# Moving the stores of the blocks' sums from SyncE to ScalarE in the edge stages of a two-layer graph kernel

## What is computed

```python
h = (x @ W).reshape(n, HEADS, OUT_C)                 # n = 6250, 8 heads of 32
e = leaky_relu(a1[src] + a2[dst], 0.2)               # 206250 edges, sorted by dst
seg_max = segment_max(e, dst, n)
ex = exp(e - seg_max[dst])
denom = segment_sum(ex, dst, n)
out = segment_sum(h[src] * (ex / denom[dst])[:, :, None], dst, n)
```

## Time and profile before

| what | value |
|---|---|
| median of the three runs | 6683.05 us |
| the profiled execution, its span | 7807.0 us |
| first edge stage's steps, by the trace | about 470 to 3178 us |
| second edge stage's steps, by the trace | about 4665 to 7084 us |
| busy over the span | PE 67%, PEld 48%, DVE 42%, POOL 46%, ACT 18% |

### The profile page before, as it was taken

The page is one execution under the profiler, slowest core; times in us unless marked ns, Lnnn a source line. Parts: engine busy times, 40 slices in busy tenths (PEclk is TensorE's granted clock), DMA queues, the critical chain, the costliest instruction groups (busy, mean ns, idle before and its releaser), DMA issues. The chain is left out here.

```text
span 7807.0 us, 99204 instructions
## 1 busy us (share of the span) xinstructions
PE 5257.7 (67%) x19729; PEld 3739.4 (48%) x19729; DVE 3278.9 (42%) x5938; ACT 1371.0 (18%) x2977; POOL 3613.4 (46%) x3708
## 2 busy tenths in 40 slices
PE   2387887788788878228999625556565556663498
PEld 1144444444444444227999514444444444442498
DVE  6255555555555555721111313333333333336244
ACT  2122222222222222002222200000000000000122
POOL 2635555555555554042222056666666666650222
PEclk9689999999999999658999857777777777786699
DMA  6434444444444443515666544444444444434255
GB/s 220 136 101 122 122 119 123 124 124 125 122 123 121 122 124 102 186 60 165 183 183 183 153 102 114 113 115 115 114 112 113 113 114 116 113 102 154 101 198 188
DMA packets 718013, 1022.24 MB, mean 131 GB/s; under 512 B 301733, under 2 KB 531561, under 8 KB 692608
## 3 DMA queue, kind: packets, MB, share of 16 engines
q0 software_dynamic: 183456, 485.95, 23.8%
q1 hardware_dynamic: 527676, 519.31, 21.7%
q10 hardware_dynamic: 6564, 14.14, 0.5%
HBM read 868.26 MB, written 153.27 MB: 131 GB/s over the span
## 5 line engine op out<-in xcount | busy, mean ns | idle before, releaser
L773 POOL DMA_INDIRECT e_rows<-sc_table,e_eidx x3224 | 3115.9, 966 | 2253.8 <-issue 952.6
L880 PE MATMUL e_ps_o<-e_rows,e_oh 128*128 128x264 f32 x6448 | 1918.5, 449 | 856.9 <-ACT e_res L969 700.8
L880 PEld LDWEIGHTS e_ps_o<-e_rows,e_oh 128*128 128x128 f32 x6448 | 1379.2, 222 | 1384.3 <-issue 1147.6
L1064 DVE SCALAR_TENSOR_TENSOR e_u<-e_encr,e_adst,e_ps_hd 128x512 f32<-128x512 f32 x806 | 597.1, 745 | 1160.2 <-remote 366.1
L1132 DVE TENSOR_TENSOR e_rows<-e_rows,e_ps_w 128x1024 f32<-128x1024 f32 x806 | 970.7, 1207 | 106.3 <-issue 83.5
L822 PE MATMUL e_ps_X<-e_u,e_hwide 128*104 128x512 f32 x1612 | 871.1, 635 | 16.8 <-DVE e_u L1064 14.8
L1055 DVE TENSOR_SCALAR e_ohT<-e_at,e_nid 96x512 bf16<-96x512 int16 x806 | 292.5, 363 | 1384.6 <-DMA e_aw<-sc_a2p 553.7
L969 ACT COPY e_res<-e_ps_o 32x264 f32<-32x264 f32 x806 | 296.0, 367 | 3291.4 <-PE e_ps_o L884 1242.4
L810 PE MATMUL e_ps_enc<-e_at,e_w_enc 96*128 96x512 bf16 x806 | 317.9, 394 | 570.6 <-ACT e_encr L942 383.4
L1676 PE MATMUL x_ps_h<-x_xT,x_w 128*128 128x256 f32 x2624 | 648.2, 405 | 15.4 <-DMA x_b<-in_L_ffn_b_dram 15.4
L1676 PEld LDWEIGHTS x_ps_h<-x_xT,x_w 128*128 128x128 f32 x2624 | 638.5, 337 | 20.6 <-issue 16.4
(11 more groups left out here) (290 smaller groups left out, 3538.7 us busy)
## 6 DMA issues: line engine op xcount, KB each, us to landing
x_w<-in_L_ffn_W_dram SPq DMA_DIRECT2D x112, 1024.0 KB
e_at<-sc_grp SPq DMA_DIRECT2D x403, 192.0 KB
x_w<-in_L_ffn_w_dram SPq DMA_DIRECT2D x60, 1024.0 KB
e_rows<-sc_table,e_eidx POOLq DMA_INDIRECT x3224
e_at<-sc_grp SPq DMA_DIRECT2D x403, 96.0 KB
sc_agg<-e_res SPq DMA_DIRECT2D x816, 33.0 KB
sc_xb<-r_zero SPq DMA_DIRECT2D x24, 1032.0 KB
x_xin<-sc_xb SPq DMA_DIRECT2D x86, 258.0 KB
```

Of the source, the lines that this page charges most:

```text
L773: pool.indirect_dma_start(rows[:, k, s, j, :], None, dr["table"][:, :], bass.IndirectOffsetOnAxis(eidx[:, k, s, j:j + 1], 0)).then_inc(s_r ...
L880: nc.tensor.matmul(ps_o[:, 0:ROW], oh[:, k, at_j:at_j + P], rows[:, k, s, j, :], start=(j == 0), stop=False)
L1064: nc.vector.scalar_tensor_tensor(u[:, p, h, :], encr[:, h, :], adst[:, h:h + 1], ps_hd[:, h, :], ALU.add, ALU.mult).then_inc(s_u, 1)
```

## The change

SP loses the store, its two holds, and the third number of each table entry. ACT gets them: after the `evict` of step s it issues the store of step s - 1, whose window start it reads from the table itself. `evict` loses its own hold on `s_out`, since that of the store now covers it. The 31 stores that followed SP's loop become one after ACT's loop.

```diff
@@ SP
             def entry(t):
-                _, vals = nc.values_load_multi_w_load_instructions(tab[0:1, bass.ds(t * 3, 3)], engines=[sp.engine], ...
+                _, vals = nc.values_load_multi_w_load_instructions(tab[0:1, bass.ds(t * 3, 2)], engines=[sp.engine], ...
-            def store(t, s, n):
-                hold(sp, s_out, t * 16 - (32 * SB - OUT0), s_ps)
-                hold(sp, s_ev, t - (BEHIND - 1 - EV0), s_ps)
-                sp.dma_start(dr["agg"][bass.ds(n, WIN), :], res[0:WIN, kept((s - BEHIND) % SB), :]).then_inc(s_out, 16)
@@ phase of SP
-                    g, n, back = entry(t)
+                    g, n = entry(t)
                     load(ring(s), g, n)
-                    store(t, s, back)
...
-            for j in range(BEHIND):
-                t = steps * (2 * SB) + (3 * SB + j)
-                _, _, back = entry(t)
-                store(t, j % SB, back)
@@ ACT
             def evict(b, s):
                 t = b * SB + s
                 hold(act, s_o, t + (1 + O0), s_pa)
-                if not isinstance(t, int) or t + BEHIND - 2 * SB + 1 >= since(s):
-                    hold(act, s_out, t * 16 + 16 * (BEHIND - 2 * SB + 2 - since(s)), s_pa)
                 nc.scalar.copy(res[0:WIN, kept(s), :], ps_o[0:WIN, 0:ROW]).then_inc(s_ev, 1)
+            def window(t):
+                _, vals = nc.values_load_multi_w_load_instructions(tab[0:1, bass.ds(t * 3 + 1, 1)], engines=[act.engine], ...
+            def store(b, s):
+                t = b * SB + s
+                hold(act, s_out, t * 16 + OUT0, s_pa)
+                hold(act, s_ev, t + (1 + EV0), s_pa)
+                act.dma_start(dr["agg"][bass.ds(window(t), WIN), :], res[0:WIN, kept(s), :]).then_inc(s_out, 16)
             def phase(b, k, pre, turn, turns):
                 m, n = b + 1, b + 2
                 for s in range(SB):
                     evict(b, s)
+                    if s > 0:
+                        store(b, s - 1)
+                    elif not isinstance(b, int) or b > 0:
+                        store(b - 1, SB - 1)
                     if first and pre:
                         relu(n, s)
```

More of the change, by code:

```diff
@@ L642, in kept @@
             return s % KEEP if s < 2 * KEEP else KEEP
-        def since(s):
-            return SB - KEEP if s < KEEP else KEEP if s < 2 * KEEP else SB
         def behind(s):
@@ L667, in entry @@
                 why = "the planning stage writes only groups and starts of windows that lie inside their arrays"
-                _, vals = nc.values_load_multi_w_load_instructions(tab[0:1, bass.ds(t * 3, 3)], engines=[sp.engine], min_val=0, max_val=NP,
+                _, vals = nc.values_load_multi_w_load_instructions(tab[0:1, bass.ds(t * 3, 2)], engines=[sp.engine], min_val=0, max_val=NP,
                                                                    skip_runtime_bounds_check_because=why)
@@ L707, in _ @@
                     sp.wait_ge(s_hd if first else s_xa, (t - behind(s) + 1) * PER)
-                g, n, _ = entry(t)
+                g, n = entry(t)
                 load(ring(s), g, n)
@@ L718, in _ @@
                     tables(2 * SB, 0)
-            sp.sem_inc(s_out, OUT0)
             steps = steps_of(sp)
@@ L740, in _ @@
                     phase(i * 2 + (1 + q), 1 - q)
-            for j in range(BEHIND):
-                t = steps * (2 * SB) + (3 * SB + j)
-                _, _, back = entry(t)
-                store(t, j % SB, back)
-            hold(sp, s_out, steps * (32 * SB) + (16 * SB + 16 * BEHIND + OUT0), s_ps)
             hold(sp, s_ei[1], steps * 16 + 32, s_ps)
@@ L966, in evict @@
                 hold(act, s_o, t + (1 + O0), s_pa)
-                if not isinstance(t, int) or t + BEHIND - 2 * SB + 1 >= since(s):
-                    hold(act, s_out, t * 16 + 16 * (BEHIND - 2 * SB + 2 - since(s)), s_pa)
                 nc.scalar.copy(res[0:WIN, kept(s), :], ps_o[0:WIN, 0:ROW]).then_inc(s_ev, 1)
+            def window(t):
+                why = "the planning stage writes only starts of windows that lie inside their arrays"
+                _, vals = nc.values_load_multi_w_load_instructions(tab[0:1, bass.ds(t * 3 + 1, 1)], engines=[act.engine], min_val=0, max_val=NP,
+                                                                   skip_runtime_bounds_check_because=why)
+                return nc.s_assert_within(vals[0], 0, NP, skip_runtime_bounds_check_because=why)
+            def store(b, s):
[3 more added lines that the diff above has]
+                act.dma_start(dr["agg"][bass.ds(window(t), WIN), :], res[0:WIN, kept(s), :]).then_inc(s_out, 16)
             def phase(b, k, pre, turn, turns):
@@ L997, in _ @@
                     relu(1, s)
+            act.sem_inc(s_out, OUT0)
             steps = steps_of(act)
@@ L1004, in _ @@
             phase(steps * 2 + 2, 0, False, False, 0)
+            store(steps * 2 + 2, SB - 1)
+            hold(act, s_out, steps * (32 * SB) + (48 * SB + OUT0), s_pa)
         @block.vector
```

## The result

The changed kernel takes 7077.53 us (median of four runs, 7072.94 to 7078.8) against 6681.52 us before: 5.96% slower, ratio 1.0596 with a 95% interval of [1.0583, 1.0609]. The forecast was 7060, the range 6850 to 7300.

The account below looks back on a forecast made before the run. TensorE was taken to bound the first edge stage, GpSimd's gathers the second. 377 first-stage steps at 1.0 us give 377 us, the second stage and SP's relief zero; from 6683 this gives 7060 us, range 6850 to 7300.

Parts of the forecast that it names:

- GpSimd hides everything in the second stage: Second edge stage: gathers set 5.0 us a step and ACT idles before its copy, so the added work costs zero.
- 1.23 us added: ACT, first stage, between copy and first ReLU: holds and address 0.48, issue 0.34, table read 0.28, its address and gap 0.13.
- 0.16 saved: ACT, first stage: `evict` loses one hold, priced at 0.16 to 0.24 us, giving net +1.07 us.
- slack of 0.1: First stage: the first ReLU has at most 0.1 us to spare before `enc` half 1, leaving about 1.0 us of delay.
- the rest behind 1.07: SP's 1.07 us from store end to next load, less half of 0.48 and a 0.715 read: address and gap, taken as 0.13.
- dear rival: First stage: 1.7 us a step, 641 us in all, and perhaps less clock for a waiting TensorE; 7320 to 7400 us, chance 0.15.
- the forecast's 377 us: First edge stage: 377 steps with copy and store ahead of their ReLUs, at 1.0 us each.
- Faster by SP's relief: Second-stage loads: late loads set the pace, so 120 waits each shrink by 0.9 us, 108 us; 6575 us, chance 0.07.
- No change: Both edge stages: GpSimd sets the pace with slack enough for 1 us a step; 6683 to 6695 us, chance 0.05.
- partly hidden: First stage: batch steps already waiting for gathers eat half the delay; 0.3 to 0.6 us a step, 6800 to 6900 us, chance 0.13.
- bound of 4030 us of gathers: GpSimd, both edge stages: 806 steps at 5.0 us of gathers each, leaving 2650 us of the median for everything else.

Follow-up runs that it names:

- e1: Changed kernel with the stores moved to ACT in the first edge stage alone, SP keeping them elsewhere: 7084.65 us, ratio 1.0598.
- e2: Changed kernel with the stores moved to ACT in the second edge stage alone, SP keeping them elsewhere: 6676.17 us, ratio 0.9992.
- e3: Changed kernel, but ACT issues the store behind the step's two ReLUs instead of ahead of them: 6658.29 us, ratio 0.9963.
- e4: Changed kernel, but ACT issues the store between the step's two ReLUs: 6618.16 us, ratio 0.99.
- e7: Kernel before, SP keeping all stores; only the copy's hold on landed stores is executed ahead of time, between the ReLUs in the first stage: 6634.21 us, ratio 0.9923.

## Why the prediction was right

- *Which stage pays.* Forecast: the first alone. Measured: 398 us there, -4 in the second, and e1 and e2 show it one at a time. That GpSimd hides everything in the second stage is right too: its batches stay at about 65 us, 13 x 4 x 1.25.
- *The path.* Forecast: copy, ReLU of half 0, `enc` half 1, with nothing beside it. e3 and e4 prove it by position: behind that ReLU the store is free, but for step 1 in e3, where the copy of the logits is on the path as well.
- *The price.* The working had 1.23 us added and 0.16 saved. Measured: the ReLU came 1.06 us later (1.34 against 0.28) and the copy 0.14 sooner (e3's 4.81 against 4.95), net 0.92, and plain steps grew by 0.93. The 0.28 of the table read (0.278) and the 0.34 of the issue (0.322) were good; the holds and addresses were overpriced by about 0.15. The slack of 0.1 does not exist. The prediction read it from the 0.14 us between the ReLU's end and `enc` half 1; but in the changed kernel, where TensorE does wait for the ReLU, the distance is the same 0.14 (1505.72 to 1505.86), and in before it is 0.14 in the median of the 377 steps and never less. So these 0.14 us lie between the ReLU's end and the start that it releases even where TensorE waits; they are no room. Two errors of like size largely cancelled. Three slips moved nothing: the rest behind 1.07 comes to 0.115 and not 0.13, the upper end of the forecast to 7173 and not 7170, and one of the 377 steps has no store ahead of its ReLUs.
- *What was missing.* 377 x 0.93 = 351 us of the 398. The rest is step 1: in the mean it grew from 7.33 to 9.89 us, 1.63 above the price of the delay, and 29 x 1.63 = 47 us. (The medians, 7.93 and 10.04, hide a part, since 12 of the 29 were short before.) The prediction had the clock as part of its dear rival, for the stage as a whole; the stage's clock fell only from 0.99 to 0.97 (window 1200 to 1600 us), in this one step it mattered. So the forecast's 377 us came near the measured 396 partly by luck: the plain steps' price was 0.07 too high, and the clock in step 1 had been put at nothing.
- *The rivals.* Faster by SP's relief: no run shows a gain by it. In the second stage e2 gives 0.9992 [0.9983, 1.0002], and in the plain steps of the first e7 and e4 are 4.81 and 4.83. No change and partly hidden: excluded by the 0.93 a step. Dearer: not reached.
- *The signs.* The ReLU at 1.34 us (forecast about 1.4), `enc` half 1 waiting 0.91 (about 1) and a plain step of 5.88 (5.8 to 5.9) came as said. One sign did not: waits on the ReLU from 700 to 2900 us were to grow to 600 us or more and came to 349.1. The 254.9 that they were to grow from belonged to the distorted execution.
- *The landing in the second stage.* The prediction has no term for it, and none shows in the time; but there the store's hold on landed stores did hold ACT up. In the changed kernel 46 of 402 copies start more than 0.3 us behind the end of their sum, up to 5.0 us, and none in before. The gathers hide it.
- *The distorted profile.* A step of 7.0 us was the distorted execution's. The bound of 4030 us of gathers against the median had shown that it could not be the runs'.
- *The Trainium skill's rules.* The prediction's sum has table read, issue and ReLU one behind the other. That fits: in the 376 steps with a store the ReLU never starts before the issue's end, in the median 0.21 us behind it.
## What to carry to other kernels

Before an instruction is put on an idle engine, look not at the engine's busy share (ACT's was 20%) but at which of its instructions the critical loop waits for, and in every kind of step. The same store cost 396 us ahead of the first ReLU and nothing behind it, yet behind both ReLUs it was 40 us dearer than between them, because in one step of 13 another instruction on the path came next. Waits count as well: a hold that was satisfied each time still took 0.14 us (the copy starts 0.273 us behind TensorE's sum with it and 0.128 without), and moved off the loop of an engine that is 95% busy (381.36 of the 400 us from 1200 to 1600) it was worth 0.8%. And compare a profile's span with the timed runs first; where they differ by 17%, profile again, or build the bounds from durations of single instructions.

## What the runs showed of the hardware

- One profiled execution of the kernel before was 17% longer than its runs, though ScalarE's copy of the sums took 0.367 us in it as against 0.368 in the second, which was not longer. What slowed that one is open.
- A table read from SBUF on a sequencer takes 0.278 us for one number on ACT and 0.63 us for two on SP, and SP's for three 0.826 us in the undistorted execution of before: 0.28 to 0.32 us a number. The Trainium skill (Runtime: NRT & Kernel Launch, Instruction fetch mechanics) gives about 200 ns per register, and speaks of loads from HBM; the numbers here grow with the count too, but are 1.4 to 1.6 times that.
- TensorE was granted either the full clock throughout or half of it for a part of the same step in different batches, with the same instructions. After it had idled 1.8 us for the ReLU and 1.1 us for the logits (changed kernel) a part of step 1 was at half in 28 of 29 batches; after 0.8 and 1.1 us (before) in 17 of 29.
